# Attention scores computed on 32-row tiles of the array instead of from masked copies of the keys

## The chip, the cores and the metric

One core of a Trainium2 chip runs the whole program. The time is the device time of one execution in microseconds (us), and the figure given for a kernel is the median of its runs. Engines are named as the profile names them: PE is TensorE's matmul, PEld its weight load, DVE is VectorE, ACT ScalarE, POOL GpSimd, SP SyncE.

## The reference, cut to what matters

Four images of 128 channels and 16x16 places pass through four layers. Layers 0 and 1 are a full attention and a convolution on the channels. Then every image is 256 tokens of 128 numbers, and two token blocks follow. Each is an attention with 8 heads of 16 numbers (the first looks back over a window of 64 tokens, the second over all earlier ones) and a feed-forward (the second one picks 2 of 8 experts). The part that the change touches is the score of each head:

```python
q = (x @ Wq.T).reshape(B, S, NHEAD, hd)          # hd = 16
scores = einsum('bhnqd,bhnkd->bhnqk', q, k) / sqrt(hd)
scores = where(valid, scores, -1e30)
attn = softmax(scores)
out = einsum('bhnqk,bhnkd->bhnqd', attn, v)
```

## The kernel before, in words

Both token attentions run as phases. `PHASES` holds four: attention 0 for images 0 and 1, attention 0 for images 2 and 3, then the same two pairs for attention 1. While one pair is in its phase, the other pair's normalization, projection out and feed-forward are done "aside". There is no scheduler: each engine's program is written out by hand in order, and semaphores tie them. An engine works strictly through its own list.

To keep more than single-pass precision, queries and keys are split into an upper and a lower part, and products are summed from the parts. `project` makes keys and queries of an image in two banks, each with two groups `g` of four heads. `queries_keys` (ACT) copies the upper parts to `k_parts` and `q_hi`; `lower_keys` and `lower_queries` (DVE) subtract. `k_parts` holds upper parts on rows 0 to 63 and lower parts on rows 64 to 127, so that one product over all 128 rows sums both. A head has only 16 of each 64 rows, so the other heads must be zero in its copy: `masked_keys` makes, for each of 8 heads, a masked copy `kM[:, h, :]` of 128 rows and 256 keys. DVE does heads 0 to 3 for the first image of the pair (L1094), ACT for the second (L450), and POOL heads 4 to 7 for both (L382).

A phase has six score units per image (`SCORE_BANKS`). A unit fills one bank of 512 columns. Four units are wide: query tile 1, 256 keys, two heads (units 0, 2, 4, 5). Two are narrow: query tile 0, 128 keys, four heads (units 1, 3). `scores` (L700, L709) fills a bank with two products of 512 columns (`q_hi`, then `q_lo`, against `kM`) and one bf16 product with the identity that adds the mask (256 columns in the wide units of attention 1). Then `largest` (DVE, L1106) takes the negated maxima, `exps` (ACT, L484) the exponentials with their sums, `turn_probs` (PE, L727) transposes, DVE (L1133) or ACT (L450) copies, and `mix` (PE, L739) multiplies with the values, each head on 32 columns of the array (a column tile).

`unit_step(a, ns, u)` sets PE's order: for each image in turn, scores of unit `u`, transposes of unit `u - 1`, mix of unit `u - 2`. In unit 1 of the later phases the scores of both images come first, then `project_out` (L759) of the other pair, then the transposes of unit 0. DVE's `units` is in the same order: the maxima of image n, then what is aside (`norm`, L1072, in unit 2), then the copy, image by image.

Of the kernel before, what the change touches and what calls it, by code (L numbers as in the profile page):

```python
# [19 lines left out]
HP = 32  # L20
# [15 lines left out]
    cq=256, ck=256, cv=128, co=256, causal0=512, causal1=512, headmask=8, router=8,  # L36
# [9 lines left out]
EARLY = AT["aq"]  # L46

# [3 lines left out]
def build(nc, x, packed, b1, b2, w1, w2, routes, out):  # L51
    with ExitStack() as ctx:
# [34 lines left out]
        def vec(i):  # L87
# [67 lines left out]
        kM = each("kM", [128, HEADS, T], F32R, n=2, scope=attention_memory)  # L155
# [9 lines left out]
        hhi = each("hhi", [128, HC, 512], F32R, n=2)  # L165
        hlo = each("hlo", [128, HC, 512], F32R, n=2)
# [4 lines left out]
        sb("rest_of_attention_memory", [128, 2 * TOK])  # L171
# [39 lines left out]
        kM_ready, kM_act_ready, kM2_ready, av_ready = (  # L211
            sem(n) for n in ("kM_ready", "kM_act_ready", "kM2_ready", "av_ready"))
# [55 lines left out]
        def other(n):  # L268
# [7 lines left out]
        SECOND_HALF = next(u for u, (_, heads) in enumerate(SCORE_BANKS) if heads[0] >= HG)  # L276

        def unit_query(u):
            return SCORE_BANKS[u][0]

        def unit_heads(u):
            return SCORE_BANKS[u][1]
# [65 lines left out]
        def _(pool):  # L348
# [29 lines left out]
            def masked_keys(a, n):  # L378

                pool.wait_ge(k_parts_ready, a * B + n + 1)  # L380
                for h in range(HG, HEADS):
                    last = G.tensor_scalar(kM[n % 2][:, h, :], k_parts[n % 2][:, h // HG, :].bitcast(F32),  # L382
                                           const("headmask", h, h + 1), 1.0, ALU.mult, ALU.mult)
                last.then_inc(kM2_ready, 1)

# [14 lines left out]
            for a, ns in PHASES:  # L400
                for n in ns:
                    masked_keys(a, n)
# [38 lines left out]
        def _(act):  # L441
# [28 lines left out]
            def masked_keys(a, n):  # L470

                act.wait_ge(k_parts_ready, a * B + n + 1)
                for h in range(HG):
                    last = copy(kM[n % 2][:, h, :], k_parts[n % 2][:, 0, :].bitcast(F32), const("headmask", h, h + 1))
                last.then_inc(kM_act_ready, 1)

            def exps(a, n, u):
# [5 lines left out]
                for i, h in enumerate(unit_heads(u)):  # L483
# [93 lines left out]
            for p, (a, ns) in enumerate(PHASES):  # L577
# [5 lines left out]
                masked_keys(a, ns[1])  # L583
# [52 lines left out]
        def _(pe):  # L636
# [47 lines left out]
            def scores(a, n, u):  # L684
                if u == 0:
                    pe.wait_ge(q_lo_ready, a * B + n + 1)
                    pe.wait_ge((kM_ready, kM_act_ready)[n % 2], (a * B + n) // 2 + 1)
                if u == SECOND_HALF:
                    pe.wait_ge(kM2_ready, a * B + n + 1)
# [5 lines left out]
                width = unit_width(u)  # L695
                i, heads = unit_query(u), unit_heads(u)
                dst = lane[n][u % 2]
                g = heads[0] // HG
# [4 lines left out]
                mask = A_MASK[a][i]  # L703
# [5 lines left out]
                mm(dst, ident_bf[:, :], mask, start=False, stop=True, skip_group_check=True).then_inc(s_full[n], 1)  # L709
# [21 lines left out]
            def mix(a, n, u):  # L731
                pe.wait_ge(pT_ready[n], a * UNITS + u + 1)
                key_tiles = unit_width(u) // 128
                for kt in range(key_tiles):
                    for i, h in enumerate(unit_heads(u)):
# [27 lines left out]
            def unit_step(a, ns, u, aside, before=None):  # L763
                if u == 1 and before is not None:
                    for n in ns:
                        scores(a, n, u)
# [4 lines left out]
                    return  # L771
                for n in ns:
                    if u < UNITS:
                        scores(a, n, u)
# [236 lines left out]
        def _(dve):  # L1011
# [64 lines left out]
            def lower_keys(a, n):  # L1076

                dve.wait_ge(k_hi_ready, a * B + n + 1)
                low = k_parts[n % 2][64:128, :, :]
                V.tensor_tensor(low, lane[n][1][64:128, :].rearrange("r (g t) -> r g t", g=2), low.bitcast(F32),  # L1080
                                ALU.subtract).then_inc(k_parts_ready, 1)

            def lower_queries(a, n):
# [3 lines left out]
                                       float(HD) ** -0.5, q_hi[n % 2][:, :, :].bitcast(F32), ALU.mult, ALU.subtract  # L1087
                                       ).then_inc(q_lo_ready, 1)

            def masked_keys(a, n):  # L1090

                dve.wait_ge(k_parts_ready, a * B + n + 1)
                for h in range(HG):
                    last = V.tensor_scalar(kM[n % 2][:, h, :], k_parts[n % 2][:, 0, :].bitcast(F32),  # L1094
                                           const("headmask", h, h + 1), None, ALU.mult)
                last.then_inc(kM_ready, 1)
# [6 lines left out]
            def largest(a, n, u):  # L1103
                dve.wait_ge(s_full[n], a * UNITS + u + 1)
                heads = unit_heads(u)
                V.tensor_reduce(negmax[n][:, unit_query(u), heads[0]:heads[-1] + 1],  # L1106
                                lane[n][u % 2][:, :].rearrange("q (h k) -> q h k", h=len(heads)),
                                AX.X, ALU.max, negate=True).then_inc(max_ready[n], 1)

            def units(a, ns, aside, a_before):  # L1110
                before = [other(n) for n in ns]
                for u in range(UNITS + 1):
                    if u == 1 and a_before is not None:
                        for n in ns:
                            largest(a, n, u)
                        for n in before:
                            add_attention(a_before, n)
                    for n in ns:
# [8 lines left out]
                        if 0 < u < UNITS and not (u == 1 and a_before is not None):  # L1127
                            largest(a, n, u)
# [187 lines left out]
            for p, (a, ns) in enumerate(PHASES):  # L1316
# [8 lines left out]
                masked_keys(a, ns[0])  # L1325
# [185 lines left out]
```

## Time and profile before

| | us |
|---|---|
| median of 3 runs | 281.54 (281.47 to 282.26) |
| the profiled execution's own time | 281.39 |
| its span | 279.6 |
| PE busy | 258.1 |
| DVE busy | 233.9 |
| ACT busy | 172.4 |
| POOL busy | 90.7 |

The granted TensorE clock is full throughout. The token attentions begin at about 42.6 us of the span (the first projections of keys) and end at about 170.5 us, where the experts' first product starts. The four phases' projections start near 42.6, 71, 104.4 and 137.5 us. A matmul's time in the trace runs from its issue to its modelled end, so matmuls overlap; the distance between two starts is the rate at which PE gets through them.

### The profile page before, as it was taken

Reading aid. Unit: us, or ns where it says so; the run is one execution under the profiler, and the core shown is the slowest. Engines: PE = TensorE matmul, PEld = TensorE weight load, DVE = VectorE, ACT = ScalarE, POOL = GpSimd, SP = SyncE. Lnnn points to the kernel's source line nnn. Section 1 sums busy time; section 2 is a strip of 40 time slices with the busy share of each in tenths; the row PEclk is TensorE's granted clock in tenths of the full one; section 3 lists DMA queues with packets and bytes.
Section 4 is the critical chain, followed back from the end, with each engine's and each line's share of the span. In section 5 each row is a group of like instructions: output and inputs, shape, how many; then the busy total and the mean of one; then the engine's idle time right before and its main releaser. Section 6 shows DMA issues by size and latency. Waiting matters only on the chain.

```text
span 279.6 us, 4798 instructions
## 1 busy us (share of the span) xinstructions
PE 258.1 (92%) x1547; PEld 182.1 (65%) x1547; DVE 233.9 (84%) x543; ACT 172.4 (62%) x489; POOL 90.7 (32%) x111
## 2 busy tenths in 40 slices
PE   7899977999998999989898999999999999999982
PEld 2777556556875658656666768678886876667661
DVE  4785589988687898969899555999999999999993
ACT  2384436778677677776776975597555491836540
POOL 5100026007401345015251200204555444445523
PEclk9999999999999999999999999999999999999999
DMA  7910000003200000000000000004413223110202
GB/s 217 372 51 2 0 1 0 2 0 89 64 1 2 2 2 0 0 2 1 4 0 0 2 2 0 0 9 163 137 46 107 75 75 97 53 75 0 76 2 75
DMA packets 9447, 12.66 MB, mean 45 GB/s; under 512 B 1865, under 2 KB 7113, under 8 KB 9297
## 3 DMA queue, kind: packets, MB, share of 16 engines
q1 hardware_dynamic: 9136, 12.18, 13.3%
q8 instruction: 12, 0.20, 0.3%
q10 hardware_dynamic: 288, 0.20, 0.2%
q14 instruction: 11, 0.08, 0.1%
HBM read 11.82 MB, written 0.56 MB: 44 GB/s over the span
## 4 chain that ended last, share of the span: by engine, by line
DVE 41%; PE 32%; issue 8%; ACT 7%; DMA 6%; POOL 2%; SPq 1%; DVEq 1%; POOLq 0%; ACTq 0%
DVE hlo L1347 9%; DVE hhi L1345 6%; PE bank L727 5%; PE bank L700 5%; PE bank L739 5%; PE bank L672 5%; DVE negmax L1106 4%; DMA b1s<-b 4%; DVE yc L1408 3%; DVE probT L1133 3%; ACT hb L601 2%; DMA pk<-packed 2%; DVE stats L1058 2%; PE bank L709 2%; POOL rstd L360 2%
## 5 line engine op out<-in xcount | busy, mean ns | idle before, releaser
L601 ACT ACTIVATE hb<-bank,b1s 128x512 f32<-128x512 f32 x64 | 42.7, 710 | 34.6 <-DMA b1s<-b 29.4
L484 ACT ACTIVATE prob<-bank,negmax 128x256 f32<-128x256 f32 (+1 forms) x128 | 52.5, 427 | 17.7 <-DVE negmax L1106 17.3
L1347 DVE TENSOR_TENSOR hlo<-hb,hhi 128x512 fp32r<-128x512 f32 x64 | 52.4, 839 | 1.9 <-ACT hhi L604 0.6
L1106 DVE TENSOR_REDUCE negmax<-bank 128x2 f32<-128x512 f32 (+1 forms) x48 | 32.6, 686 | 12.2 <-PE bank L709 11.9
L395 POOL TENSOR_TENSOR w_lo<-w_raw,w_hi 128x512 fp32r<-128x512 f32 x16 | 23.9, 1498 | 39.9 <-DVE w_hi L1397 26.2
L428 POOL TENSOR_TENSOR acc<-acc,yc 128x512 f32<-128x512 f32 x16 | 24.2, 1521 | 30.8 <-DVE yc L1408 30.8
L727 PE MATMUL bank<-pk,prob 128*128 128x128 f32 x192 | 29.4, 278 | 2.2 <-ACT prob L484 1.6
L360 POOL TENSOR_TENSOR rstd<-ve,neghalf 128x2 f32<-128x2 f32 x16 | 11.5, 729 | 56.9 <-DVE ve L1067 56.9
L1345 DVE CAST hhi<-hb 128x512 fp32r<-128x512 f32 x32 | 28.7, 898 | 0.0
L962 PE MATMUL bank<-hhi,w_hi 128*128 128x512 f32 x64 | 26.0, 406 | 1.4 <-DVE hhi L1345 1.1
L965 PE MATMUL bank<-hlo,w_hi 128*128 128x512 f32 x64 | 27.0, 421 | 0.0
L484 ACT ACTIVATION_READ_ACCUMULATOR prob<-bank,negmax 128x1 f32 x128 | 26.9, 210 | 0.0
L948 PE MATMUL bank<-xhi,w_hi 128*128 128x512 f32 x64 | 26.0, 407 | 0.8 <-ACT hhi L604 0.6
L727 PEld LDWEIGHTS bank<-pk,prob 128*128 128x128 f32 x192 | 22.0, 142 | 6.3 <-ACT prob L484 3.7
L739 PE MATMUL bank<-probT,vh 128*32 128x128 f32 x384 | 25.8, 280 | 0.1
L949 PE MATMUL bank<-xlo,w_hi 128*128 128x512 f32 x64 | 25.4, 397 | 0.0
L950 PE MATMUL bank<-xhi,w_lo 128*128 128x512 f32 x64 | 25.4, 396 | 0.0
L963 PE MATMUL bank<-hhi,w_lo 128*128 128x512 f32 x64 | 25.4, 396 | 0.0
L700 PE MATMUL bank<-kM,q_hi 128*128 128x512 f32 x48 | 23.9, 497 | 1.3 <-DVE kM L1094 1.3
L604 ACT ACTIVATE hhi<-bank,b1s 128x512 fp32r<-128x512 f32 x32 | 22.6, 707 | 0.0
L450 ACT ACTIVATE probT<-bank 128x512 f32<-128x512 f32 x28 | 16.8, 604 | 5.3 <-PE bank L727 5.0
L739 PEld LDWEIGHTS bank<-probT,vh 128*32 128x32 f32 x384 | 14.0, 108 | 8.1 <-issue 7.7
(157 smaller groups left out, 501.0 us busy)
## 6 DMA issues: line engine op xcount, KB each, us to landing
w_raw<-w SPq DMA_DIRECT2D x16, 256.0 KB, 3.1
comb_b<-routes SPq DMA_DIRECT2D x8, 512.0 KB, 3.8
pk<-packed SPq DMA_DIRECT2D x1, 2188.0 KB, 11.1
pk<-packed SPq DMA_DIRECT2D x1, 560.0 KB, 6.3
out<-acc SPq DMA_DIRECT2D x4, 128.0 KB, 1.8
xs<-x SPq DMA_DIRECT2D x3, 128.0 KB, 2.7
xs<-x ACTq DMA_DIRECT2D x1, 128.0 KB, 2.9
b1s<-b SPq DMA_DIRECT2D x8, 2.0 KB, 3.5
```

The source lines that it names most:

```text
L484: last = nc.scalar.activation(prob[n][:, u % 2, i * width:(i + 1) * width], lane[n][u % 2][:, i * width:(i + 1) * width], ACT.Exp, bias=ne ...
L601: nc.scalar.activation(hb[i % 2][:, j, :], h_bank[j][:, :], ACT.Relu, bias=b1s[s][:, j:j + 1]).then_inc(h_ready, 1)
L700: mm(dst[:, :], part[n % 2][:, g, i * 128:(i + 1) * 128], kM[n % 2][:, heads[0]:heads[-1] + 1, 0:width], start=(part is q_hi), stop=False, ...
L727: last = nc.tensor.transpose(lane[n][2][:, i * 128:(i + 1) * 128], prob[n][:, u % 2, i * 128:(i + 1) * 128], ident)
L739: last = mm(lane[n][3][HP * r:HP * r + HP, col:col + 128], vh[n][:, kt, h, :], probT[n][:, u % 2, at:at + 128], start=(kt == 0), stop=(kt ...
L948: mm(h_bank[j][:, :], w_hi[s][:, 0, chunk], xhi[:, cols], start=True, stop=False)
L949: mm(h_bank[j][:, :], w_hi[s][:, 0, chunk], xlo[:, cols], start=False, stop=False)
L962: mm(y_bank[i % 2][:, :], w_hi[s][:, 1, chunk], hhi[i % 2][:, j, :], start=(j == 0), stop=False)
L965: last = mm(y_bank[i % 2][:, :], w_hi[s][:, 1, chunk], hlo[i % 2][:, j, :], start=False, stop=(j == HC - 1))
L1106: V.tensor_reduce(negmax[n][:, unit_query(u), heads[0]:heads[-1] + 1], lane[n][u % 2][:, :].rearrange("q (h k) -> q h k", h=len(heads)), A ...
L1345: V.tensor_copy(hhi[i % 2][:, j, :], hb[i % 2][:, j, :]).then_inc(hhi_ready[1], 1)
L1347: V.tensor_tensor(hlo[i % 2][:, j, :], hb[i % 2][:, j, :], hhi[i % 2][:, j, :].bitcast(F32), ALU.subtract).then_inc(hlo_ready, 1)
```

## The change

The weights of the queries and keys are laid out so that head `h` has 32 rows of its own in each group: 16 rows that will be the upper part, then 16 for the lower. Row `r` (0 to 3) and group `g` belong to head `head_of(g, r)`. Signs and zeros in a column of constants (`rowsign`) make `k_parts` and the queries come out so that a product over a head's 32 rows is the wanted sum. The masked copies and `kM` go. A head's score is now two products (`q_hi`, `q_lo`) over 32 rows, placed at a row tile of the array. An image with an odd number takes the neighbouring row (`r ^ 1`), so the two images of a pair use different rows, and their products are issued in turn. The mask product comes first. A bank is filled by one row at a time: in a narrow unit, the second row's products wait until the first row's have ended (`rows_done`). For unit 0 each image's scores are issued by themselves.

```diff
-        SCORE_BANKS = ((1, range(0, 2)), (0, range(0, 4)), (1, range(2, 4)),
-                       (0, range(4, 8)), (1, range(4, 6)), (1, range(6, 8)))
+        SCORE_UNITS = ((1, (0,)), (0, (0, 1)), (1, (1,)), (0, (2, 3)), (1, (2,)), (1, (3,)))
+        def unit_rows(n, u):
+            return sorted(r ^ (n % 2) for r in SCORE_UNITS[u][1])
+        def unit_heads(n, u):
+            return [head_of(g, r) for r in unit_rows(n, u) for g in range(2)]
...
 (ACT, queries_keys)
-                copy(q_hi[n % 2][:, :, :], lane[n][0][:, :].rearrange("r (g t) -> r g t", g=2), float(HD) ** -0.5
+                copy(q_hi[n % 2][:, :, :], lane[n][0][:, :].rearrange("r (g t) -> r g t", g=2), const("rowsign", 1, 2)
 (POOL, ACT, DVE)
-            def masked_keys(a, n):
...
 (PE)
-            def scores(a, n, u):
...
-                for part in (q_hi, q_lo):
-                    mm(dst[:, :], part[n % 2][:, g, i * 128:(i + 1) * 128],
-                       kM[n % 2][:, heads[0]:heads[-1] + 1, 0:width],
-                       start=(part is q_hi), stop=False, skip_group_check=True)
...
+                mm(dst, ident_bf[:, :], mask, start=True, stop=False, skip_group_check=True)
+
+            def scores(a, ns, u):
+                for n in ns:
+                    masked(a, n, u)
+                i, width = unit_query(u), unit_width(u)
+                row_count = len(SCORE_UNITS[u][1])
+                for at in range(row_count):
+                    for n in ns:
+                        if at:
+                            pe.wait_ge(rows_done[n], 2 * a + (u + 1) // 2)
+                    for part in (q_hi, q_lo):
+                        for g in range(2):
+                            for n in ns:
...
+                                last = mm(lane[n][u % 2][:, col:col + width],
+                                          part[n % 2][rows, g, i * 128:(i + 1) * 128],
+                                          k_parts[n % 2][rows, g, 0:width],
+                                          start=False, stop=(part is q_lo), tile_position=(HP * r, 0),
+                                          skip_group_check=True)
...
 (PE, unit_step)
+                if 0 < u < UNITS:
+                    scores(a, ns, u)
                 for n in ns:
-                    if u < UNITS:
-                        scores(a, n, u)
+                    if u == 0:
+                        scores(a, (n,), u)
...
 (DVE, lower_keys: one subtraction over all 128 rows, with a row's sign; units)
+                    elif 0 < u < UNITS:
+                        for n in ns:
+                            largest(a, n, u)
                     for n in ns:
...
-                        if 0 < u < UNITS and not (u == 1 and a_before is not None):
-                            largest(a, n, u)
```

On DVE the maxima of both images now come ahead of everything else of a unit. The waits of PE on the masked copies (`kM_ready`, `kM_act_ready`, `kM2_ready`) go with them. The experts' buffers are laid out anew in the memory that `kM` leaves.

## Rows read from the trace of the kernel before

**Rows 1.** The page's head: busy us (share) and instructions of each engine.

```profile
PE 258.1 (92%) x1547; PEld 182.1 (65%) x1547; DVE 233.9 (84%) x543; ACT 172.4 (62%) x489; POOL 90.7 (32%) x111
```

**Rows 2.** Stretches: us, busy PE, PEld, DVE, ACT, POOL, granted clock, DMA share, GB/s.

```profile
51.00:70.90 19.90, 19.20 (x159) 11.55 (x158) 16.49 (x35) 16.61 (x72) 5.24 (x4) 1.00 0.14 42
...
80.00:88.00 8.00, 6.62 (x49) 4.90 (x49) 7.44 (x23) 5.53 (x27) 1.39 (x2) 1.00 0.00 1
88.00:104.40 16.40, 15.79 (x140) 10.14 (x139) 13.57 (x36) 11.89 (x45) 5.76 (x8) 1.00 0.01 3
```

**Rows 3.** Chain that ended last, start of the first phase: start us, us, what.

```profile
46.03 0.70 DVE k_parts L1080
...
46.76 1.92 DVE kM L1094 x4
...
48.82 0.70 PE bank L700 x2
```

**Rows 4.** Groups of instructions by form: busy us, mean ns; idle before.

```profile
L382 POOL TENSOR_SCALAR kM<-k_parts,pk 128x256 fp32r<-128x256 f32 x32 | 15.3, 498 | 12.0 <-DVE k_parts L1080 12.0
...
L1094 DVE TENSOR_SCALAR kM<-k_parts,pk 128x256 fp32r<-128x256 f32 x16 | 7.4, 521 | 0.1
...
L450 ACT ACTIVATE kM<-k_parts,pk 128x256 fp32r<-128x256 f32 x16 | 6.8, 498 | 0.0
L450 ACT ACTIVATE hT<-bank 128x256 f32<-128x256 f32 x16 | 6.0, 384 | 5.9 <-PE bank L649 5.9
```

**Rows 5.** PE in order of time, one image's step: start us, us, what.

```profile
98.42 0.43 PE L739 MATMUL bank<-probT,vh 128*32 128x128 f32 x8
98.77 0.50 PE L700 MATMUL bank<-kM,q_hi 128*128 128x512 f32 x1
99.11 0.39 PE L700 MATMUL bank<-kM,q_lo 128*128 128x512 f32 x1
99.35 0.39 PE L709 MATMUL bank<-band_bf,ident_bf 128*128 128x512 bf16 x1
99.58 0.60 PE L727 MATMUL bank<-pk,prob 128*128 128x128 f32 x4
100.11 0.43 PE L739 MATMUL bank<-probT,vh 128*32 128x128 f32 x8
```

**Rows 6.** PEld in order of time, the same step.

```profile
98.42 0.16 PEld L739 LDWEIGHTS bank<-probT,vh 128*32 128x32 f32 x8 [0.17 <-issue]
...
98.88 0.19 PEld L700 LDWEIGHTS bank<-kM,q_lo 128*128 128x128 f32 x1
```

**Rows 7.** In order of time, second phase: a run of loads, a run of fp32 products.

```profile
76.46 1.06 PE L680 MATMUL bank<-pk,hT 128*128 128x128 f32 x8
...
80.53 1.86 PEld L759 LDWEIGHTS bank<-pk,attnT 128*128 128x128 f32 x16 [0.50 <-DVE attnT L1161]
```

**Rows 8.** In order of time, units 0 and 1 of the second phase.

```profile
77.27 0.48 PE L700 MATMUL bank<-kM,q_hi 128*128 128x512 f32 x1
...
78.26 0.69 DVE L1106 TENSOR_REDUCE negmax<-bank 128x2 f32<-128x512 f32 x1 [0.24 <-PE bank L709]
...
79.79 1.28 DVE L1161 TENSOR_TENSOR attnT<-bank,rT 128x512 f32<-128x512 f32 x2
...
80.53 2.05 PE L759 MATMUL bank<-pk,attnT 128*128 128x128 f32 x16 [0.21 <-DVE attnT L1161]
...
82.19 0.93 DVE L1166 TENSOR_TENSOR t<-bank,t 128x256 f32<-128x256 f32 x2
```

**Rows 9.** In order of time, unit 2 of the second phase.

```profile
85.94 0.69 DVE L1106 TENSOR_REDUCE negmax<-bank 128x2 f32<-128x512 f32 x1
86.73 0.60 DVE L1072 TENSOR_SCALAR ht<-t,mv,rstd 128x128 f32<-128x128 f32 x2
87.25 0.68 DVE L1106 TENSOR_REDUCE negmax<-bank 128x2 f32<-128x512 f32 x1
...
87.48 0.41 PE L649 MATMUL bank<-pk,ht 128*128 128x128 f32 x2 [1.00 <-DVE ht L1072]
```

More of the change, by code:

```diff
@@ L46, with head_of @@
 EARLY = AT["aq"]
+def head_of(g, r):
+    return HG * g + (r + 2 * g) % HG
 GAMMA, BETA, BQ, BK, BV, BP, BSQ, BCONV = range(8)
@@ L209, in build @@
             sem(n) for n in ("aqk_full", "k_hi_ready", "q_hi_ready", "k_parts_ready", "q_lo_ready", "atv_full"))
-        kM_ready, kM_act_ready, kM2_ready, av_ready = (
-            sem(n) for n in ("kM_ready", "kM_act_ready", "kM2_ready", "av_ready"))
+        av_ready, rows_done = sem("av_ready"), sems("rows_done")
         av_full, rb_ready, rT_full, rT_ready, attn_ready, wo_full, t_ready = (
@@ L270, in other, with unit_maxima @@
             return (n + 2) % B
-        SCORE_BANKS = ((1, range(0, 2)), (0, range(0, 4)), (1, range(2, 4)),
-                       (0, range(4, 8)), (1, range(4, 6)), (1, range(6, 8)))
-        SECOND_HALF = next(u for u, (_, heads) in enumerate(SCORE_BANKS) if heads[0] >= HG)
+        SCORE_UNITS = ((1, (0,)), (0, (0, 1)), (1, (1,)), (0, (2, 3)), (1, (2,)), (1, (3,)))
         def unit_query(u):
-            return SCORE_BANKS[u][0]
-        def unit_heads(u):
-            return SCORE_BANKS[u][1]
+            return SCORE_UNITS[u][0]
+        def unit_rows(n, u):
+            return sorted(r ^ (n % 2) for r in SCORE_UNITS[u][1])
+        def unit_heads(n, u):
+            return [head_of(g, r) for r in unit_rows(n, u) for g in range(2)]
+        def unit_maxima(n, u):
+            rows = unit_rows(n, u)
+            of_rows = negmax[n][:, unit_query(u), :].rearrange("q (a b) -> q b a", b=2)
+            return of_rows[:, rows[0] % 2:rows[0] % 2 + len(rows), slice(0, 4, 3) if rows[0] < 2 else slice(1, 3)]
         def unit_width(u):
@@ L376, in lower_tokens @@
                                 ).then_inc(xlo01_ready, 1)
-            def masked_keys(a, n):
[L380 to L384, printed above, removed]
             for j in range(2):
@@ L482, in exps @@
                 width = unit_width(u)
-                for i, h in enumerate(unit_heads(u)):
+                for i, h in enumerate(unit_heads(n, u)):
                     last = nc.scalar.activation(
@@ L708, in scores @@
                     dst, mask = dst[:, :], mask[:, :]
-                mm(dst, ident_bf[:, :], mask, start=False, stop=True, skip_group_check=True).then_inc(s_full[n], 1)
+                mm(dst, ident_bf[:, :], mask, start=True, stop=False, skip_group_check=True)
+            def scores(a, ns, u):
+                for n in ns:
+                    masked(a, n, u)
+                i, width = unit_query(u), unit_width(u)
+                row_count = len(SCORE_UNITS[u][1])
[6 more added lines that the diff above has]
+                            for n in ns:
+                                place = at if n % 2 == 0 else row_count - 1 - at
+                                r = unit_rows(n, u)[place]
+                                rows = slice(HP * r, HP * r + HP)
+                                col = (2 * place + g) * width
+                                last = mm(lane[n][u % 2][:, col:col + width],
[3 more added lines that the diff above has]
+                                          skip_group_check=True)
+                                if (part, g) == (q_lo, 1):
+                                    last.then_inc(s_full[n] if at == row_count - 1 else rows_done[n], 1)
             def turn_probs(a, n, u, aside):
@@ L734, in mix @@
                 for kt in range(key_tiles):
-                    for i, h in enumerate(unit_heads(u)):
+                    for i, h in enumerate(unit_heads(n, u)):
                         g, r = divmod(h, HG)
@@ L771, in unit_step @@
                     return
+                if 0 < u < UNITS:
+                    scores(a, ns, u)
                 for n in ns:
-                    if u < UNITS:
-                        scores(a, n, u)
+                    if u == 0:
+                        scores(a, (n,), u)
                     for job, at in ((turn, TURN_STEP), (product, PRODUCT_STEP)):
@@ L1086, in lower_queries @@
                 V.scalar_tensor_tensor(q_lo[n % 2][:, :, :], lane[n][0][:, :].rearrange("r (g t) -> r g t", g=2),
-                                       float(HD) ** -0.5, q_hi[n % 2][:, :, :].bitcast(F32), ALU.mult, ALU.subtract
+                                       const("rowsign", 1, 2), q_hi[n % 2][:, :, :].bitcast(F32), ALU.mult, ALU.subtract
                                        ).then_inc(q_lo_ready, 1)
[L1090 to L1096, printed above, removed]
             def copy_values(a, n):
@@ L1450, in padded_rows, with by_rows @@
         return r.reshape(2, 128, 128).transpose(1, 0, 2).reshape(128, 256)
-    def twice(w):
-        return np.concatenate([w[:, 0:64], w[:, 0:64], w[:, 64:128], w[:, 64:128]], axis=1)
+    def by_rows(w):
+        return np.concatenate([w[:, HD * head_of(g, r):HD * head_of(g, r) + HD]
+                               for g in range(2) for r in range(HG) for _ in range(2)], axis=1)
     vecs = np.zeros((128, 8), f32)
@@ L1478 @@
     ch = np.arange(128)
+    rowsign = np.zeros((128, 8), f32)
+    low = ch % HP >= HD
+    rowsign[:, 0] = low
+    rowsign[:, 1] = np.where(low, f32(HD) ** -0.5, -f32(HD) ** -0.5)
     parts = dict(
```

43 lines of the change are left out of this document (13 added, 30 removed).

## Prediction

> **What bounds the kernel now.** I read the page's head first: PE is busy 92% of the span, DVE 84%, and ACT and POOL have room [rows 1]. The masked copies that go are work of DVE, ACT and POOL, so the question is where those engines set the end. I then read the busy time stage by stage [rows 2]. From 51 us to the end of the first phase PE is busy 19.20 of 19.90 us; in the later units of the second phase, 15.79 of 16.40. There PE sets the pace. Between, from 80 to 88 us, it is DVE: 7.44 of 8.00, while PE has 6.62. The third and fourth phases look like the second. Last I read the chain of waits at the head of the first phase: it runs through the four DVE copies of `kM`, 1.92 us, before PE's first score [rows 3]. In the other phases the same copies lie under PE's projections, its last mix, the transposes of the inverse sums and the values: PE's eight passes of the values start at 76.46, 0.11 apart [rows 7], which brings it to 77.3, and the first score is at 77.27 [rows 8]: no wait.
>
> So the change takes its work from engines that wait for PE in most places, and gives PE another form of the same products. PE's price for a unit decides.
>
> **What is removed.** 16 copies on DVE (521 ns), 16 on ACT (498 ns) and 32 on POOL (498 ns) [rows 4], 7.4, 6.8 and 15.3 us of busy time. In the first phase the path gets shorter: the second image's lower keys end at 46.73, its four passes for the values take PE 0.44 after that, and scores could start near 47.25 instead of 48.82 [rows 3], 1.55 us earlier. DVE would then do the normalization of images 2 and 3 some 1.4 us earlier, and unit 0's maxima with it. I take -1.4 us. In the other three phases: nothing, PE covers it. POOL has nothing late behind its copies: the power of the norms waits for DVE's variances.
>
> **What is added beside PE.** `q_hi`'s scale becomes a column of constants; ACT's copy with such a scale takes 498 ns for 256 columns where one with a fixed scale takes 384 [rows 4], at most 0.11 us in each of 8 copies, under PE's projections. `lower_keys` works on all 128 rows instead of 64, at the same columns: nothing.
>
> **PE's price of a unit.** In a step of one image [rows 5] the starts lie 0.34 (`q_hi`), 0.24 (`q_lo`) and 0.23 (mask) apart. A 512-column product costs about 0.235 us when its load is hidden, three of them 0.70, and the first pays 0.10 more: it follows a mix on column tiles, and its load wasn't ahead. The second load, at 98.88, did lie under the product before it [rows 6]. So a change of tile form costs 0.10 (a load laid bare). In a pair of images a score step costs 2 x 0.70 = 1.40 beside those.
>
> Now the new unit. Each product over 32 rows needs its own load of 128 columns: 4 per image in a wide unit (256 columns each), 8 in a narrow one (128 columns each), where before there were 2. The streamed columns are the same: 1,024 per image. How fast 128-column loads follow each other is in a run of 16: (1.86 - 0.19) / 15 = 0.11 us [rows 7]. A product of 256 columns is half of the 512-column one, 0.11 as well; one of 128 columns would be 0.055. Whether two row tiles overlap no row shows. The nearest are the column tiles: eight fp32 passes on four of them start and end within 0.35 us (98.42 to 98.77), and their 8 loads take 0.16 in all [rows 5, 6], while 8 passes of the same 128 columns on the full array take (1.06 - 0.28) / 7 = 0.11 each, 0.89 [rows 7]. So tiles do run side by side there. I take it that rows do too: two images' products as a pair, each pair at the slower of its load and its stream.
> - Wide unit, two images: 2 masks 0.47, change of form 0.10, 4 pairs 0.44, change back 0.10: 1.11, or **-0.29** against 1.40.
> - Narrow unit: 0.47 + 0.10 + 8 pairs bound by loads 0.88 + 0.10, and the wait for `rows_done`. That is PE waiting for its own last product: 0.27 us to its end (of four 128-column ones that take 0.60, starts 0.11 apart [rows 5]), 0.14 from a releaser's end to the product that waited (48.68 to 48.82 [rows 3]), less the 0.11 that a pair would have taken: 0.30. In all 1.85, **+0.45**.
> - Unit 0, image by image on a single row tile: 0.235 + 0.10 + 4 x 0.11 + 0.10 = 0.88, +0.18 if loads hide under the product on the same rows; +0.5 if each of the last three is bare. I take **+0.25** an image.
>
> A phase: 3 x -0.29 + 2 x 0.45 + 2 x 0.25 = +0.53 of PE. Ends: with the loads of neighbouring tiles overlapping too, so that a narrow pair streams in 0.055, -0.44 for each narrow unit; with nothing overlapping, +0.44 for each wide and +0.88 for each narrow one.
>
> The Trainium skill, "TensorE: Matmul & The Clock Gate", section "LDWEIGHTS", says a load's time goes by its columns and not its rows, so a 32-row load is as long as a full one; that speaks against this change, which makes 32 loads of an image's 12 in a phase (4 x 4 + 2 x 8, for 6 x 2). No run here shows it yet: the trace has 128-column loads on full rows alone. By the page a load costs the full 0.11 as in my sum; were it priced by rows, 0.03, a narrow unit would be bound by its stream, 0.44 less. Its Part 3 says a load overlaps a product in flight only on other rows; here the full array's load at 98.88 did overlap [rows 6], and by the page unit 0 would cost the +0.5.
>
> **Where it lands.** First phase: -1.4, +0.5 for unit 0 (already partly in DVE's shadow, 0.3 stays), then PE-bound +0.03 (3 wide, 2 narrow): -1.1. Phases two to four: unit 0 and the first narrow unit push `project_out` from 80.53 to about 81.1 [rows 8], DVE's residual behind it by as much: +0.5. In unit 2, DVE now takes both maxima before both norms. Until now one maximum (0.69) lay in the gap in which POOL makes `rstd`, then the norm at 86.73, then the other maximum; PE waited 1.00 us for that norm [rows 9]. The second maximum ahead of it makes the norm 0.6 us later, and with it the turn and all that PE has queued behind it (transposes of unit 1, mix of unit 0, then unit 3). PE's own saving of 0.29 there doesn't help. +0.5. Units 3 to 5: +0.45 - 2 x 0.29 = -0.13. At the phase's end the second image's last maxima come earlier, since its last scores no longer stand behind the first one's transposes and mix: -0.3. A phase: +0.57, three +1.7. Sum: +0.6, on 281.39, so **282.0** (the median of the runs, 281.54, lies 0.15 above the profiled execution; I leave that in the rounding).
>
> **The rivals.** Within 0.3% (0.8 us) counts as no change here.
> - *A. As above.* Its own range is 280.2 to 284, by the choice for unit 0, 0.3 around the self-wait, and whether the norm's delay is real. Chance 0.40.
> - *B. The 128-column products are slow.* The full-rate products of this format all have 512 columns; nothing shows 128. If such a short one ran like plain fp32, it would take 2 x 0.11 = 0.22 instead of hiding under a 0.11 load [rows 7]: 8 pairs x 0.11 = +0.88 a narrow unit, 8 such units, 7.0, nine tenths on the path: +6.3, **288.3**. For it: short operands are what no row vouches for. Against: the columns streamed are the same. Chance 0.25.
> - *C. Row tiles do not overlap*, or their loads queue one by one. +0.44 x 3 + 0.88 x 2 = 3.1 a phase, 12.3, on the path 11: **293**. Against it stand the column tiles. Chance 0.12.
> - *D. Faster.* The loads of two row tiles overlap as those of the column tiles do (8 in 0.16), so that a narrow pair costs 0.055, not 0.11: -0.44 in each of 8 narrow units, -3.5. This one mechanism gives **278.5**. It decides from about 0.08 a pair on: 8 x 8 x 0.03 = 1.9 is enough to be under 280.7. Chance 0.23. The skill's "TensorEngine Tiling (Array Packing)", "Key Properties", says that tiles load and multiply in parallel, which would be this case; no row shows it for rows.
>
> **How the numbers follow.** Faster by over 0.3% (under 280.7): D, and 0.06 of A, 0.29. Within 0.3%: 0.18 of A. Slower: the rest, 0.53. The range 278 to 289.5 holds A, B and most of D, leaving out C and the ends of D and B.
>
> **What would show it.** Pairs of L700's successor: starts 0.11 apart for two images in wide units (A), 0.055 apart a pair in narrow ones (D), 0.22 (B), or 0.11 per single product (C). A gap of 0.3 to 0.4 in the middle of a narrow unit. First score of the first phase near 47.3 us. Phases two to four longer by 0.5 and the wait before the turn in unit 2 near 1.5 us. The prediction is wrong if a narrow unit costs less than 1.4 or over 2.3 us, or if phase lengths move where PE has not.

## The result, and the profile after

The changed kernel takes 299.84 us (median of 4 runs, 295.96 to 303.33) against 281.53. The ratio is 1.060 (95% interval 1.050 to 1.070); ratios here leave out runs that lay more than 1.5% above the fastest of the same kernel, so they are a little below the quotient of the medians. The prediction was 282.0, in a range of 278 to 289.5. The profiled execution took 299.37, its span is 18.0 us longer than before, and the runs of this kernel spread over 7 us where those of before lay within one.

The page's head and its row of the granted clock:

```profile
span 297.6 us, 5034 instructions
PE 269.0 (90%) x1695; PEld 192.9 (65%) x1707; DVE 228.6 (77%) x527; ACT 166.2 (56%) x473; POOL 75.4 (25%) x79
...
PEclk9999999999999998777999975999999999999997
```

DVE, ACT and POOL have less to do than in [rows 1], as the change says. PE has more, in part because it is no longer at full clock throughout.

The four phases as stretches (columns as in [rows 2]), each from its first projection of keys to the next one's; before, they took 28.27, 33.31, 33.11 and 33.20 us, all at a granted clock of 1.00:

```profile
43.70:70.78 27.08, 25.66 (x231) 17.80 (x232) 23.17 (x55) 19.94 (x77) 6.58 (x6) 1.00 0.11 33
70.78:107.20 36.42, 31.06 (x284) 22.26 (x285) 26.25 (x66) 21.89 (x80) 7.09 (x10) 1.00 0.02 7
107.20:148.79 41.59, 35.98 (x283) 26.65 (x284) 27.08 (x69) 22.06 (x80) 7.10 (x10) 0.84 0.01 2
148.79:188.43 39.64, 35.26 (x307) 26.05 (x309) 21.75 (x51) 22.88 (x84) 2.80 (x4) 0.87 0.00 1
```

The first phase is 1.2 us shorter. The second is 3.1 longer at full clock. The third and fourth are 8.5 and 6.4 longer, and there the clock is down: what they lose beyond the second phase's 3.1, 5.4 and 3.3 us, is the clock's part, if the rest costs them the same. That is an estimate by subtraction. With 1.1 us by which the first phase starts later (the profiled executions of all kernels here have it between 42.4 and 43.7) this makes 17.9 of the 18.0.

What a lower clock does to one group, the projection out, in the third and in the fourth phase:

```profile
117.52 3.78 PE L768 MATMUL bank<-pk,attnT 128*128 128x128 f32 x16
...
158.66 2.05 PE L768 MATMUL bank<-pk,attnT 128*128 128x128 f32 x16
```

The same 16 passes take 3.78 us at half clock and 2.05 at full, as in [rows 8].

The second phase's waits of PE (total us, times, longest), in its stretch:

```profile
PE bank L642 <- DVE ht L1082: 1.6, 1, 1.6
PE bank L736 <- DVE fy L1127: 1.2, 1, 1.2
PE bank L653 <- DVE probT L1136: 0.8, 1, 0.8
PE bank L736 <- DVE probT L1136: 0.6, 1, 0.6
```

4.2 us in these four, where the kernel before waited 2.0 in all of its second phase, 1.00 of it in the wait of [rows 9]. How one of them comes about, in order of time; the first two rows are DVE, the third PE:

```profile
96.03 1.29 DVE L1108 TENSOR_REDUCE negmax<-bank 128x2 f32<-128x512 f32 x2 [0.87 <-PE bank L712]
97.24 0.41 DVE L1127 TENSOR_TENSOR fy<-bank,pk 128x256 f32<-128x256 f32 x1
...
97.80 0.63 PE L736 MATMUL bank<-pk,prob 128*128 128x128 f32 x4 [1.16 <-DVE fy L1127]
```

DVE itself waits 0.87 us for the scores of both images, does both maxima, and only then the copy `fy` that empties the bank of the other pair's feed-forward. PE's transposes want that bank.

### The profile page after: what moved, and what is told of

It is laid out like the page before. It is cut to its first block, busy times and chain, and to the rows that moved or that the text cites. A ratio compares the mean times of both kernels' runs of the same rounds, so it can differ in the third digit from the quotient of the medians.

```text
span 297.6 us, 5034 instructions
## 1 busy us (share of the span) xinstructions
PE 269.0 (90%) x1695; PEld 192.9 (65%) x1707; DVE 228.6 (77%) x527; ACT 166.2 (56%) x473; POOL 75.4 (25%) x79
## 4 chain that ended last, share of the span: by engine, by line
DVE 40%; PE 40%; issue 7%; ACT 6%; DMA 3%; POOL 1%; DVEq 1%; POOLq 0%; SPq 0%; ACTq 0%
DVE hlo L1349 8%; PE bank L712 7%; DVE hhi L1347 6%; DVE negmax L1108 6%; PE bank L736 5%; PE bank L748 4%; PE bank L665 4%; DVE yc L1410 3%; PE bank L768 3%; PE bank L692 2%; DMA b1s<-b 2%; DVE probT L1136 2%; DVE stats L1068 2%; DVE ht L1082 1%; PE bank L759 1%
## 5 line engine op out<-in xcount | busy, mean ns | idle before, releaser
L1108 DVE TENSOR_REDUCE negmax<-bank 128x2 f32<-128x512 f32 (+1 forms) x48 | 31.3, 686 | 25.1 <-PE bank L712 24.9
L736 PE MATMUL bank<-pk,prob 128*128 128x128 f32 x192 | 34.0, 307 | 6.0 <-DVE fy L1127 2.3
L736 PEld LDWEIGHTS bank<-pk,prob 128*128 128x128 f32 x192 | 23.5, 155 | 13.0 <-issue 8.7
L478 ACT ACTIVATION_READ_ACCUMULATOR prob<-bank,negmax 128x1 f32 x128 | 27.5, 215 | 0.0
L748 PE MATMUL bank<-probT,vh 128*32 128x128 f32 x384 | 26.7, 298 | 0.0
L1136 DVE COPY probT<-bank 128x512 f32<-128x512 f32 x24 | 16.0, 685 | 6.2 <-PE bank L736 6.0
```

The lines of the kernel that those rows point to most:

```text
L478: last = nc.scalar.activation(prob[n][:, u % 2, i * width:(i + 1) * width], lane[n][u % 2][:, i * width:(i + 1) * width], ACT.Exp, bias=ne ...
L736: last = nc.tensor.transpose(lane[n][2][:, i * 128:(i + 1) * 128], prob[n][:, u % 2, i * 128:(i + 1) * 128], ident)
L748: last = mm(lane[n][3][HP * r:HP * r + HP, col:col + 128], vh[n][:, kt, h, :], probT[n][:, u % 2, at:at + 128], start=(kt == 0), stop=(kt ...
L1108: V.tensor_reduce(unit_maxima(n, u), lane[n][u % 2][:, :].rearrange("q (b a k) -> q b a k", a=2, k=unit_width(u)), AX.X, ALU.max, negate=T ...
```

## The experiments

**DVE's order put back.** The maxima return to their old place among DVE's instructions; PE is as changed.

```diff
-                    elif 0 < u < UNITS:
-                        for n in ns:
-                            largest(a, n, u)
                     for n in ns:
                         ...
+                        if 0 < u < UNITS and not (u == 1 and a_before is not None):
+                            largest(a, n, u)
```

> The changed kernel, with DVE's maxima back in their old places (image by image, behind the feed-forward's copy and ahead of the norm); PE's order stays as changed. Theory 1 (the order costs: PE's turn and transposes wait for DVE work that now stands behind two maxima, and the idle PE then loses its clock): the waits of 1.6, 0.8 and 1.2 us in phases two to four shrink to those of before, the clock stays full, 281 to 284 us. Theory 2 (products over 32 of the 128 rows lower the granted clock by themselves): the clock still drops in phases three and four, 288 us or more.

285.69 us (284.49 to 290.13), ratio 1.011 (1.007 to 1.016). Most of the loss is gone with one edit on DVE. The second phase, still at full clock, went from 36.42 us to 34.48, where the kernel before has 33.31:

```profile
69.33:103.81 34.48, 31.25 (x286) 22.32 (x285) 26.15 (x66) 22.00 (x80) 7.11 (x10) 1.00 0.03 9
```

But the clock still fell, for a short stretch in phase three and a longer one in phase four, in an execution of 290.13. Neither theory had this right alone (theory 1: PE's waits cost the clock; theory 2: products over 32 rows do).

**Image by image.** As the last, and PE's scores are issued for one image at a time.

```diff
-                if 0 < u < UNITS:
-                    scores(a, ns, u)
                 for n in ns:
-                    if u == 0:
+                    if u < UNITS:
                         scores(a, (n,), u)
... (unit 1 of the later phases alike; DVE's order as in the last run)
```

> As the run before, and PE too goes image by image: no two images' products in turn, so all products of an image run on one row tile after another. If neighbouring row tiles overlapped in the changed kernel, a wide unit costs 0.4 us more here and a narrow one 0.9 for a pair of images, some 10 us in all: near 292. If they did not overlap, the time is that of the run before.

323.25 us (313.08 to 334.68), far slower than the 292 expected. The first phase, at full clock, took 31.24 us against the last run's 26.94. I put these 4.3 us down to lost overlap. One image's wide unit in it (the mask, two times two products, then the next operation):

```profile
65.58 0.39 PE L692 MATMUL bank<-band_bf,ident_bf 128*128 128x512 bf16 x1
65.90 0.50 PE L712 MATMUL bank<-k_parts,q_hi 32*128 32x256 f32 x2
66.24 0.39 PE L712 MATMUL bank<-k_parts,q_lo 32*128 32x256 f32 x2
66.57 0.66 PE L736 MATMUL bank<-pk,prob 128*128 128x128 f32 x4
```

0.34 us for two products, where the changed kernel takes the same for four (below): row tiles do overlap. What came on top is the clock, in stretches in which PE hardly waits:

```profile
84.00:87.00 3.00, 2.94 (x12) 2.51 (x12) 1.03 (x2) 1.51 (x8) 0.00 (x0) 0.50 0.00 0
```

**The order without the row tiles.** The kernel before, with its masked copies, and the scores and maxima of both images ahead of the rest of a unit.

```diff
+                if 0 < u < UNITS:
+                    for n in ns:
+                        scores(a, n, u)
                 for n in ns:
-                    if u < UNITS:
+                    if u == 0:
                         scores(a, n, u)
...
+                    elif 0 < u < UNITS:
+                        for n in ns:
+                            largest(a, n, u)
                     for n in ns:
...
-                        if 0 < u < UNITS and not (u == 1 and a_before is not None):
-                            largest(a, n, u)
```

> The kernel before with its masked copies, but with the changed order on PE and DVE (the scores of both images, and their maxima, ahead of the rest of a unit). Theory 1: it is slower by what the order costs, 3 us a phase in phases two to four, 9 us or more if the clock drops as well: 290 to 298. Theory 2: the order costs little, 282 to 285, and the clock stays full.

286.34 us (285.87 to 287.25), ratio 1.016 (1.013 to 1.020). Its waits in the second phase are of the same kind, the longest as long, and by the page's row of the clock nothing moved:

```profile
PE bank L649 <- DVE ht L1075: 1.6, 1, 1.6
PE bank L727 <- DVE fy L1128: 0.8, 1, 0.8
```

```profile
PEclk9999999999999999999999999999999999999998
```

So the order costs 4.5 us of span with full-row products (284.1 against 279.6): phases two to four take 35.18, 34.88 and 34.83 us, 1.9, 1.8 and 1.6 more than before, and the first takes 27.60, 0.7 less. Such waits beside full-row products did not lower the clock: it is between 0.994 and 0.997 in the four runs.

**Waits filled.** The changed kernel, with products of zeros where PE waits.

```diff
                     if u >= 2:
                         mix(a, n, u - 2)
+                    if aside and n == ns[0]:
+                        keep_clock(lane[n][(u + 1) % 2], {2: 6, 3: 3, 4: 3}.get(u, 0))
```

> The changed kernel with products of zeros (bf16, 512 columns, results unused) on PE where it waits in units 2, 3 and 4 of phases two to four: 6, 3 and 3 of them. Theory 1: the activity in the waits keeps the clock at full, and the 9 us lost to the clock in phases three and four come back, less up to 1 us a phase for fillers that are longer than the wait: 289 to 293. Theory 2: the clock still drops, 300 or more.

293.89 us (292.25 to 297.51), ratio 1.037 (1.033 to 1.042). 6 us came back, from doing more on PE. The mean granted clock of the profiled execution went from 0.954 to 0.980, but not to full. It fell once in each of phases two to four, and always at the same place: as the other pair's projection out begins, right behind unit 0 and the first narrow unit. There are no fillers there, and no wait over 0.2 us in the 3 us before. Three waits of 1.0 to 1.2 us were left later in the phases, and it did not fall in them:

```profile
79.78 3.52 PE L768 MATMUL bank<-pk,attnT 128*128 128x128 f32 x16
...
117.53 3.68 PE L768 MATMUL bank<-pk,attnT 128*128 128x128 f32 x16
...
155.23 3.65 PE L768 MATMUL bank<-pk,attnT 128*128 128x128 f32 x16
```

These projections take 2.05 us at full clock. So the waits are not the whole cause either.

**The products by themselves.** The kernel before, and after its last product PE runs stretches of products whose results nobody reads.

```diff
+            full_rows()                      # 44 products, 128 rows, 512 columns
+            for tiles_in_turn in (1, 2, 4):
+                row_tiles(tiles_in_turn, 110)  # 32 rows, 256 columns, on 1, 2 or 4 row tiles
+                full_rows()
```

The comments in this edit and the next are not in the kernels.

> The kernel before, and after its last product PE runs stretches of about 10 us by themselves, with no waits, on real data and with results unused: 44 products over all 128 rows (512 columns); 110 over rows 0 to 31 (256 columns); 44 full; 110 pairs on two row tiles in turn; 44 full; 110 rounds over all four row tiles; 44 full. Theory 2 (products over 32 rows count for less in the clock gate): in the stretch on one row tile the granted clock falls to 0.5 though PE never waits, and comes back in the full stretch behind it; with two tiles it may fall too, with four it stays at 1. Theory 1 (only waits cost the clock): 1.0 throughout. Pairs start every 0.11 us at full clock, as single products do.

PE in order of time (start us, us, what), then two pieces of the stretch on one row tile (the third column from the end is the granted clock):

```profile
284.12 20.19 PE L1020 MATMUL bank<-xhi 32*128 32x256 f32 x110
304.24 12.61 PE L1014 MATMUL bank<-xhi 128*128 128x512 f32 x44
316.79 13.46 PE L1020 MATMUL bank<-xhi 32*128 32x256 f32 x220
330.18 10.29 PE L1014 MATMUL bank<-xhi 128*128 128x512 f32 x44
340.39 13.46 PE L1020 MATMUL bank<-xhi 32*128 32x256 f32 x440
```

```profile
286.00:288.00 2.00, 2.00 (x19) 2.00 (x18) 0.00 (x0) 0.00 (x0) 0.00 (x0) 1.00 0.00 0
290.00:292.00 2.00, 2.00 (x12) 2.00 (x11) 0.00 (x0) 0.00 (x0) 0.00 (x0) 0.50 0.00 0
```

The single products on one tile start 0.12 us apart while the clock is full (286.01, 286.13, 286.25 and so on; the 19 of the first piece count those still under way at its ends too); then the clock falls to 0.50 with PE waiting for nothing, stays there to the end of the stretch, and comes back within the full-row stretch behind it. 110 pairs on two tiles take 13.46 us, 0.122 a pair, and 110 rounds on four tiles the same, both at 1.00 throughout. So two and four tiles overlap wholly, their loads too, and of these forms the one that lowers the clock is products on a single row tile. This shows theory 2 for that form, in one execution.

**The shapes of the units by themselves.** The same, with the shapes that the kernel issues.

```diff
+            row_tiles((0, 1), 128, 110)      # pairs of 128 columns alone
+            full_rows()
+            for _ in range(14):              # unit 0, one image
+                masks((0,))
+                row_tiles((0,), 256, 4)
+            full_rows()
+            for _ in range(10):              # a wide unit, two images
+                masks((0, 1))
+                row_tiles((0, 1), 256, 4)
+            full_rows()
+            for _ in range(7):               # a narrow unit, two images
+                masks((0, 1))
+                row_tiles((0, 1), 128, 8)
```

> The kernel before, and after its last product PE runs by itself, without waits, results unused, full stretches of 44 products between them: 110 pairs of 128-column products on two row tiles; 14 times a mask and four 256-column products on one row tile (unit 0's shape); 10 times two masks and four pairs of 256 columns (a wide unit's shape); 7 times two masks and eight pairs of 128 columns (a narrow unit's shape). Theory 2 in the form that matters here: the shape of unit 0 lowers the clock, the wide shape doesn't. If the narrow pairs lower it as well, pairing unit 0 cannot be enough. If none of the shapes lowers it, the shapes alone don't do it and the waits between them are needed. Pairs of 128 columns start every 0.07 us if loads of two tiles overlap, every 0.11 if not.

The four stretches in that order, and a piece of the first at full clock:

```profile
284.95:304.54 19.59, 19.59 (x222) 19.47 (x221) 0.00 (x0) 0.00 (x0) 0.00 (x0) 0.61 0.01 2
317.48:336.15 18.67, 18.20 (x68) 11.68 (x69) 0.00 (x0) 0.00 (x0) 0.00 (x0) 0.66 0.00 1
348.57:360.43 11.86, 11.70 (x99) 6.36 (x99) 0.00 (x0) 0.00 (x0) 0.00 (x0) 1.00 0.01 1
370.78:381.58 10.80, 10.48 (x123) 7.45 (x124) 0.00 (x0) 0.00 (x0) 0.00 (x0) 1.00 0.01 2
...
285.00:288.00 3.00, 3.00 (x55) 3.00 (x56) 0.00 (x0) 0.00 (x0) 0.00 (x0) 1.00 0.02 5
```

Pairs of 128 columns without masks lose the clock, and so does unit 0's shape, masks included. The wide and the narrow unit of two images, with masks, keep it. Two things are not as in the kernel: the masks here are zeros, and all have 512 columns, while the wide units of attention 1 (phases three and four) have masks of 256. That shape was not tried. A narrow pair takes 0.11 us (55 products in 3.00 us), the price of one load of 128 columns as in the sum, not the 0.055 of a stream.

**Unit 2's norm alone.** The changed kernel, with the norm of unit 2 between the two maxima again.

```diff
-                    elif 0 < u < UNITS:
+                    elif 0 < u < UNITS and not (aside and u == NORM_STEP):
...
                         if u == NORM_STEP and aside:
+                            largest(a, n, u)
                             norm(aside, other(n))
```

> The changed kernel with one edit: in unit 2 the norm stands between the two maxima again, as before; everything else as changed. It is the one wait of the order that was priced. If that wait is all that the order costs at full clock, this is the time of the run with the whole DVE order put back, 285.7; if the feed-forward's copy and the transposes' copies behind the maxima in units 3 and 4 matter as much, about half of the way: 292 to 296.

296.08 us (295.30 to 299.01), ratio 1.053 (1.046 to 1.060). This was the wait that the prediction priced. It fell from 1.6 to 1.2 us in the second phase, and the other three of that phase stayed at 1.2, 0.8 and 0.6. The phase, at full clock, took 36.00 us: 0.4 less, of the 1.9 that DVE's whole order brings there. In all, 3.8 us came back of 14: the waits in units 3 and 4 matter more.

**Unit 0 paired.** DVE's order put back, and unit 0 too issued for both images in turn.

```diff
-                if 0 < u < UNITS:
+                if u < UNITS:
                     scores(a, ns, u)
                 for n in ns:
-                    if u == 0:
-                        scores(a, (n,), u)
```

> The changed kernel with DVE's order put back and with unit 0 too issued for both images in turn. A pair of images' unit 0 costs 2 x 0.98 in the trace and a paired wide unit 1.20: 0.76 less in each of four phases, on PE's path at the phase's start; and fewer products run on one row tile alone, which by theory 2 helps the clock. 282 to 284 against 285.7.

286.35 us (285.16 to 287.87), ratio 1.017 (1.012 to 1.022): no gain over 285.69. The saving on PE turned into a wait. PE's masks of unit 1 now stood 0.8 us in each of three phases for the second image's values, which DVE copies only after the first image's maxima. And though no product runs on a single row tile any more, the clock still fell in the profiled execution (285.59), in the second phase, behind this wait and the narrow unit:

```profile
80.00 3.54 PE L768 MATMUL bank<-pk,attnT 128*128 128x128 f32 x16
```

**The same with fillers** in the waits of units 2 and 3 (4 and 2 products of zeros).

> As e7, with products of zeros in the waits that are left in units 2 and 3 of phases two to four (4 and 2 of them). Theory 2 with waits adding to it: the clock stays full in most runs and the fillers, lying in waits, cost little: 281 to 283, and less spread between runs than e7.

286.26 us (284.96 to 289.15), ratio 1.016 (1.009 to 1.024). Nothing changed against the run without them, and the expected 281 to 283 was missed. The wait for the values was still there, and the clock still fell, once in the first phase and once in the fourth.

**Values first.** As "unit 0 paired", and DVE copies the values of both images ahead of both first maxima.

```diff
                 for n in ns:
                     copy_values(a, n)
+                for n in ns:
                     largest(a, n, 0)
```

> As the run with unit 0 paired, and DVE copies the values of both images ahead of both first maxima: PE's masks of unit 1 waited 0.8 us in each of phases two to four for the second copy. 2.4 us less than 286.35 if that wait was on the path: 283.5 to 284.5; no change if DVE, busy from there on, sets the pace anyway.

283.24 us over 10 runs, ratio 1.002 (0.998 to 1.006). The wait was on the path: at the same mean clock, 0.990, two of these runs take 282.7 us where two of "unit 0 paired" take 285.2 and 285.6. But the runs reach from 280.94 to 290.02. In the profiled one (285.84) the clock fell three times. The first, in order of time:

```profile
119.92 0.66 PE L642 MATMUL bank<-pk,ht 128*128 128x128 f32 x2 [1.53 <-DVE ht L1080]
120.37 1.06 PE L736 MATMUL bank<-pk,prob 128*128 128x128 f32 x4
```

The wait of unit 2, 1.53 us, and right behind it four transposes that take 1.06 us where they take 0.60 at full clock [rows 5].

**The narrow unit's own wait covered.** As the last, and between the two rows of a narrow unit PE does the first image's transposes, or in unit 1 of phases two to four its projection out.

```diff
                 for at in range(row_count):
+                    if at and between:
+                        between()
... (unit_step hands over what is put between)
```

> As the run before, and between the two rows of a narrow unit, where PE waits for its own products, it does the first image's transposes (in unit 1 of phases two to four, its projection out). The wait costs 0.3 to 0.4 us in each of 8 narrow units, and the extra change of form 0.1: 1.5 to 2 us less than the run before, near 282, no slower and hardly faster than the kernel before the change.

288.95 us (287.61 to 291.98), ratio 1.025 (1.019 to 1.030), 6 us slower instead of 2 faster. What was put between has waits of its own, and the second row of scores now stood behind them (from 60 to 200 us):

```profile
PE bank L770 <- DVE attnT L1163: 2.6, 3, 0.9
PE bank L738 <- DVE t L1168: 2.1, 3, 0.7
```

The two pieces, transposes and projection, were moved together, so the transposes alone were not tried.

**Values first, waits filled.** Unit 0 paired, values first, and 5 and 2 products of zeros in units 2 and 3 of phases two to four.

> The run with unit 0 paired and the values first (283.24 in the middle, 280.94 to 290.02, the spread being the granted clock), with products of zeros in the waits of units 2 and 3 of phases two to four (5 and 2). If those waits, together with the 32-row products around them, are what lets the clock fall, the runs draw together at 281 to 282.5, the kernel before. If the fall comes from the units themselves, the spread stays and the middle is 283 to 285.

281.69 us over 12 runs (280.63 to 283.23), ratio 0.999 (0.997 to 1.001). The spread shrank from 9 us to 2.6, about that of the kernel before (281.34 to 284.34 in the 17 runs beside it), and the middle by 1.5. PE no longer waits for the norm but for 1.2 us in all:

```profile
PE bank L642 <- DVE ht L1082: 1.2, 4, 0.3
```

This is the best version with row tiles here, and it is the kernel before to within what can be measured. None beat it. In its profiled execution the clock was full in all four phases, and they took 26.34, 33.96, 33.67 and 33.27 us: 1.9 less than before in the first, 1.3 more in the other three. The clock fell only after them, in the experts' stage, which took 1.9 us more than before. That it is the fillers that drew the runs together is likely, not shown: this run and the one without fillers were taken on different chips.

## Why the prediction was wrong, step by step

**PE's prices held.** In the changed kernel at full clock, PE in order of time: a narrow unit of both images up to the operation behind it, then a wide unit.

```profile
89.31 0.61 PE L692 MATMUL bank<-band_bf,ident_bf 128*128 128x512 bf16 x2
89.85 0.44 PE L712 MATMUL bank<-k_parts,q_hi 32*128 32x128 f32 x4
90.12 0.38 PE L712 MATMUL bank<-k_parts,q_lo 32*128 32x128 f32 x4
90.69 0.44 PE L712 MATMUL bank<-k_parts,q_hi 32*128 32x128 f32 x4 [0.18 <-PE bank L712]
...
91.28 0.44 PE L642 MATMUL bank<-pk,ht 128*128 128x128 f32 x2
...
100.24 0.60 PE L692 MATMUL bank<-band_bf,ident_bf 128*128 128x512 bf16 x2
100.77 0.50 PE L712 MATMUL bank<-k_parts,q_hi 32*128 32x256 f32 x4
101.12 0.40 PE L712 MATMUL bank<-k_parts,q_lo 32*128 32x256 f32 x4
101.44 0.66 PE L736 MATMUL bank<-pk,prob 128*128 128x128 f32 x4
```

The narrow unit takes 1.97 us (predicted 1.85), the wide one 1.20 (1.11). Unit 0 takes 0.98 an image, 0.28 more than the 0.70 of before (I took 0.25). The gap in the middle of the narrow unit is there: 0.57 us from 90.12 to 90.69 for two pairs that otherwise take 0.22, so 0.35 of waiting (I took 0.30). The rule of the Trainium skill ("TensorE: Matmul & The Clock Gate", Part 3) that a load overlaps a product in flight only on other rows is not borne out: on one tile alone products of 256 columns start every 0.12 us, about the price of a load or of a stream (0.11 each) but not of both. The Trainium skill's rule that a load's time goes by columns (same page, section "LDWEIGHTS") agrees: a narrow pair takes 0.11. Rival B (short products slow), C (no overlap of row tiles) and D (loads shorter on two tiles) are refuted by the same rows and by the stretches alone.

**The first phase's number held, in part by luck:** -1.2 us measured, -1.1 predicted. PE's first product on a row tile starts at 48.78 us, 5.1 after the phase's start, with its mask ahead of it, where the first score stood 6.2 after it. So the masked copies did leave the path as forecast. But the new order alone, with the masked copies kept, already makes this phase 0.7 shorter (27.60 us), and the sum held nothing for that.

**The step that failed in size: the order, "+0.57" a phase.** The second phase, at full clock, lost 3.1. For DVE's order I followed only the norm of unit 2, and that wait did grow from 1.00 to 1.59. For units 3 to 5 I wrote "-0.13", from PE's prices alone, without asking what DVE's maxima had been put ahead of there: the copies of the transposes (0.8 and 0.6 us of PE's time) and of the feed-forward's result (1.2). Putting back DVE's order alone took the phase from 36.42 to 34.48 us, so 1.9 of the 3.1 are DVE's, where I had 0.5. The 1.2 that remain stand against 0.07 in the sum without the norm. About 0.5 of them is unit 0, as the sum had it (paired, with the values first, the phase takes 33.96); what the sum took off elsewhere, 0.13 and 0.3, is not seen. PE waits there 0.6 us for ACT's exponentials and 0.4 for a copy of the transposes, and where the rest goes stays open. With the full-row products the whole order costs 1.6 to 1.9 a phase. A likely reason for the dearer waits with row tiles, not tested, is that a pair of images' scores then end together and both maxima wait for them.

**The step that was missing: the clock.** The prediction took full clock as given; some 8.7 us of the 18.0 are the clock's. That is what is left when phases three and four are charged the second phase's 3.1; the order alone, at full clock, does cost the three phases nearly the same (1.9, 1.8 and 1.6). The stretches alone show that products on one row tile, and pairs of 128 columns without masks, can lose the clock without any wait, and that unit 0's shape does. In the kernel the profiled executions show two places where it falls. In the changed kernel's it falls four times:

```profile
116.47 0.69 PE L712 MATMUL bank<-k_parts,q_hi 32*128 32x128 f32 x4 [0.18 <-PE bank L712]
...
126.91 0.66 PE L642 MATMUL bank<-pk,ht 128*128 128x128 f32 x2 [1.64 <-DVE ht L1082]
...
133.68 1.22 PE L653 MATMUL bank<-w_eff,hT 128*128 128x128 f32 x4 [0.79 <-DVE probT L1136]
...
175.39 0.87 PE L736 MATMUL bank<-pk,prob 128*128 128x128 f32 x3 [1.01 <-DVE lg L1182]
```

The first fall is in the first narrow unit behind unit 0, with no wait over 0.24 us in the 3 us before it (the row takes 0.44 at full clock). The other three are inside waits of 1.64, 0.79 and 1.01 us. The two kinds come apart in the other runs. With fillers in units 2 to 4, only the first kind is left, once a phase. With unit 0 paired and PE waiting 0.8 us for the values behind it, the first kind is still there. With unit 0 paired and the values first, but the waits unfilled, the first kind is gone and the falls stand behind waits (1.53 us, then 0.43 twice, the last some 3 us before). With unit 0 paired, the values first and the waits filled, the four phases show none. And with the same kind of waits beside full-row products there was none either. So here it took products over few rows, and waits added to it. These are single executions, and which share of the 8.7 belongs to which place stays open, since the spread from execution to execution is as large as the parts.

**The rival on the other side** (faster by loads that overlap) had its mechanism half right: loads of different row tiles do overlap, four of them in 0.122 us. But a narrow pair still costs one tile's load, 0.11, and not its stream.

## What to carry to other kernels

When instructions are moved on one engine, list for every place what they now stand ahead of and who waits for that; the dearest place may not be the one that was looked at. A product on a quarter of the rows is not only no faster than a full one: issued alone it can cost the clock, and what TensorE does behind it then takes up to twice as long (3.78 us for 2.05 here). Judge such a kernel by several runs and by the granted clock of each stretch. Use row tiles only where two or more run at once, and even then look at the clock: pairs of 128 columns by themselves lost it.

## What the runs showed of the hardware that was not expected

- Products over 32 of 128 rows on a single row tile, issued every 0.12 us with no wait, let the granted clock fall from 1.00 to 0.50 (2.4 to 1.2 GHz); the same products on two or four row tiles in turn did not, at 256 columns. At 128 columns two tiles did (0.61 over the stretch), and with two masks of 512 columns ahead of every eight pairs they did not.
- Products on two and on four row tiles cost the same, 0.122 us a round of 256 columns, loads included.
- A product of 256 columns on a single row tile, with a load of its own, costs 0.12 us, so its load does lie under the product before it on the same rows.
- PE can be over 97% busy by the profile and at half clock: 2.94 of 3.00 us in the kernel that goes image by image.
